# Second cross attention: the probability turn moved from TensorE to VectorE 32x32 transposes and SBUF-to-SBUF DMAs, attended values one context later

## The reference, cut to what matters

```
q, k, v = x @ Wq + bq,  ctx @ Wk + bk,  ctx @ Wv + bv      # 64 queries, 512 keys per context
score   = q k^T / sqrt(32) + mask * -1e9                    # per head: 64 x 512
attn    = softmax(score)                                    # over the 512 keys
x       = x + (attn v, heads side by side) @ Wo + bo
```

## Time and profile before

| what | value |
|---|---|
| median of three runs | 1252.92 us (1252.54 to 1254.14) |
| span of the profiled execution | 1248.6 us |
| TensorE busy | 1202.0 us (96%) |
| VectorE busy | 708.9 us (57%) |
| ScalarE busy | 520.2 us (42%) |
| GpSimd busy | 141.5 us (11%) |
| DMA traffic | 88.21 MB in 48485 packets, mean 71 GB/s |
| span of the 16 contexts, first score to last attended value | 399.7 to 881.8 us |

### The profile page before, as it was taken

How to read it: one execution, slowest core, us unless ns; L and a number is a source line. 1 busy time by engine, 2 the same in 40 slices (tenths; PEclk the granted TensorE clock), 3 DMA queues, 4 the chain that set the end, 5 groups by cost and what they waited for, 6 DMA issues and landing times.

```text
span 1248.6 us, 25643 instructions
## 1 busy us (share of the span) xinstructions
PE 1202.0 (96%) x10969; PEld 895.9 (72%) x10969; DVE 708.9 (57%) x1569; ACT 520.2 (42%) x1028; POOL 141.5 (11%) x164
## 2 busy tenths in 40 slices
PE   7999889999999999999999999999899999999997
PEld 5654478766466777777777777777787678888886
DVE  5456486767783555555555555555686755434432
ACT  3344447742132554545444444445453332222321
POOL 1300031166523000000000000000131100000000
PEclk9999999999999999999999999999999999999999
DMA  9669500201113110000010011110500201111210
GB/s 357 255 234 407 200 1 1 76 1 41 62 55 131 51 54 35 35 35 35 35 35 35 35 44 38 57 37 2 86 1 1 77 1 34 34 35 34 68 34 34
DMA packets 48485, 88.21 MB, mean 71 GB/s; under 512 B 19002, under 2 KB 20076, under 8 KB 44148
## 3 DMA queue, kind: packets, MB, share of 16 engines
q1 hardware_dynamic: 47024, 85.48, 19.4%
q10 hardware_dynamic: 1348, 1.09, 0.4%
HBM read 65.59 MB, written 20.97 MB: 69 GB/s over the span
## 4 chain that ended last, share of the span: by engine, by line
PE 88%; DVE 6%; ACT 3%; issue 1%; POOL 1%; DMA 1%; POOLq 0%; SPq 0%; DVEq 0%; ACTq 0%
PE bank L289 59%; PE bank L245 4%; PE bank L1790 3%; PE bank L1811 2%; PE bank L559 2%; PE bank L577 2%; PE bank L1138 2%; PE bank L1117 2%; PE bank L235 1%; DVE W L1380 1%; PE bank L495 1%; PE bank L2535 1%; PE bank L1086 1%; PE bank L1070 1%; PE bank L1094 1%
## 5 line engine op out<-in xcount | busy, mean ns | idle before, releaser
L2023 ACT ACTIVATE W<-W,low 128x512 f32<-128x512 f32 x128 | 90.9, 713 | 57.2 <-DVE low L1929 57.2
L2003 ACT ACTIVATE K<-bank,vecT 128x512 f32<-128x512 f32 x64 | 43.8, 689 | 167.0 <-PE bank L289 167.0
L225 POOL TENSOR_TENSOR rstd<-rstd,half_pow 128x1 f32<-128x1 f32 x48 | 30.9, 645 | 684.0 <-DVE rstd L221 684.0
L1902 DVE TENSOR_TENSOR W<-bank,vecT 128x256 f32<-128x256 f32 x16 | 6.8, 425 | 164.2 <-PE bank L1811 164.2
L1929 DVE CUSTOM_DVE_ANT_0 W<-bank,W 128x512 f32<-128x512 f32 x128 | 80.8, 687 | 30.6 <-PE bank L1790 30.6
L289 PE MATMUL bank<-xT,wT 128*128 128x512 f32 x384 | 92.8, 391 | 0.8 <-ACT W L2837 0.5
L289 PE MATMUL bank<-ctxT,Wkv 128*128 128x512 f32 x384 | 93.5, 396 | 0.0
L289 PE MATMUL bank<-Wq,Wkv 128*128 128x512 f32 x384 | 93.0, 394 | 0.0
L289 PE MATMUL bank<-Wkv,ctxT 128*128 128x512 f32 x384 | 92.9, 394 | 0.0
L289 PE MATMUL bank<-Wkv,Wq 128*128 128x512 f32 x384 | 92.1, 395 | 0.0
L289 PE MATMUL bank<-woT,hR 128*128 128x512 f32 x384 | 91.7, 394 | 0.1
(11 more groups left out here) (343 smaller groups left out, 2171.4 us busy)
## 6 DMA issues: line engine op xcount, KB each, us to landing
W<-ctx_turned SPq DMA_DIRECT2D x16, 1024.0 KB, 4.8
W<-in_ctx_dram SPq DMA_DIRECT2D x8, 1024.0 KB, 10.6
ctx_turned<-ctxT SPq DMA_DIRECT2D x8, 1024.0 KB, 7.6
ctx_turned<-W SPq DMA_DIRECT2D x8, 1024.0 KB, 6.6
XT<-in_ctx_dram SPq DMA_DIRECT2D x4, 1024.0 KB, 11.7
XT<-in_L_ffn_wi_dram SPq DMA_DIRECT2D x4, 1024.0 KB, 5.9
XT<-in_L_ffn_wo_dram SPq DMA_DIRECT2D x4, 1024.0 KB, 5.1
raw_own<-in_ctx_dram SPq DMA_DIRECT2D x3, 1024.0 KB, 10.7
```

The costliest lines, as they stand in the source:

```text
L225: pool.tensor_tensor(rstd[:, g:g + 1], rstd[:, g:g + 1], half_pow[:], ALU.pow).then_inc(rstd_ok.s, 1)
L2003: act.activation(K[:, m, :], bank[:, n % 4, :], ACT.Identity, bias=pcol("L1_xattn_bk", m)).then_inc(ring_a.s, 1)
L2023: act.activation(PR[:, j, :], PR[:, j, :], ACT.Exp, bias=low[:, j:j + 1], scale=-1.0, accum_out=total[:, j:j + 1]).then_inc(expd.s, 1)
```

## The change

1. TensorE no longer turns the probabilities: `probs_pe`, `turned_a` and their semaphores go. ScalarE's 8 copies per context go with them.
2. VectorE's 8 multiplications by the reciprocal per context go to GpSimd (`tensor_scalar`, 128x512). The 8 reciprocals of one column become 2 of four columns (`recips_v`).
3. VectorE turns each probability tile in place, in blocks of 32x32 (`dve.transpose`, 8 of 128x512 per context, in `probs_v`).
4. SP moves the blocks to their partitions: `move_probs(i, half)` issues 16 DMAs per half, 32 per context. Each takes 32 partitions and 16 runs of 32 elements (128 bytes) on each, from `PR` to `PT`: 512 runs and 64 KB per DMA, 2 MB per context. `scores_v(i + 1, 0)` and `(i + 1, 4)` on VectorE and `attend_pe(i)` on TensorE wait for them.
5. `attend_pe(i)` moves into the next pass, behind `scores_pe(i + 1, 1)`. Values get a second buffer (`slot(3)`). After the loop come rows, `key_weight_pe` and `attend_pe(15)`, which waits for the last 32 DMAs.
6. The order is adapted: the output stands behind the last values, `halves_a` and `halves_v` stand later in the pass, the bias additions on GpSimd stand behind the scaling of context 0, and `L1_attn_Wk` is loaded in the last context, into `V`. SP issues `load_context(i + 2)` ahead of `move_probs(i, ...)`, after it has waited for `context_v(i + 1, 3)`.

```diff
             USES = [("key", 0, m) for m in range(C)]
             for i in range(NI):
-                USES += [("value", i, k) for k in range(2)]
+                USES += [("value", i, 0)]
+                if i:
+                    USES += [("attended", i - 1, 0)]
+                USES += [("value", i, k) for k in range(1, KT)]
                 if i and i % 2 == 0:
                     USES += [("output", i // 2 - 1, 0)]
-                USES += [("value", i, k) for k in range(2, KT)]
                 if i < NI - 1:
                     USES += [("key", i + 1, m) for m in range(C)]
-                    USES += [("attended", i, 0)]
...
+            def move_probs(i, half):
+
+                sp.wait_ge(probs.s, probs(XPAIRS * i + 4 * half + 3))
+                if i:
+                    sp.wait_ge(ring.s, ring(use_of["attended", i - 1, 0]))
+                pairs = slice(4 * half, 4 * half + 4)
+                for q in range(4):
+                    rows, to = slice(32 * q, 32 * q + 32), slice(32 * q, 32 * q + 32)
+                    for r in range(4):
+                        strip = slice(32 * r, 32 * r + 32)
+                        sp.dma_start(PT[strip, pairs, :, to].rearrange("p t k n -> p (t k) n"),
+                                     PR[rows, pairs, :].rearrange("p t (k n) -> p (t k) n", n=P)[:, :, strip]
+                                     ).then_inc(pt_in[half].s, 16)
...
-                for i in range(1, NI - 1):
-                    sp.wait_ge(ctx_v.s, ctx_v(4 * i + 3))
-                    load_context(i + 1)
-                sp.wait_ge(ctx_v.s, ctx_v(4 * (NI - 1) + 3))
-                load_slot(4, "L1_attn_Wv")
-                sp.wait_ge(pt_pe.s, pt_pe(2 * NI - 1))
+                for i in range(NI):
+                    if i < NI - 1:
+                        sp.wait_ge(ctx_v.s, ctx_v(4 * (i + 1) + 3))
+                        if i < NI - 2:
+                            load_context(i + 2)
+                        else:
+                            load_slot(4, "L1_attn_Wv")
+                    else:
+                        sp.wait_ge(ring.s, ring(use_of["attended", i - 1, 0]))
+                        sp.dma_start(V[:], a["L1_attn_Wk"].rearrange("(c p) n -> p c n", p=P)).then_inc(slot_in[3].s, 16)
+                    for half in range(2):
+                        move_probs(i, half)
+                for half in range(2):
+                    probs_landed(sp, NI - 1, half)
                 load_slot(5, "L1_attn_Wq")
...
+                for i in range(NI):
+                    for t in range(XPAIRS):
+                        if t % 4 == 0:
+                            pool.wait_ge(recip.s, recip(2 * i + t // 4))
+                        pool.tensor_scalar(PR[:, t, :], PR[:, t, :], total[:, t:t + 1], None, ALU.mult).then_inc(scaled_p.s, 1)
...
                     scores_pe(i, 1)
+                    if i:
+                        attend_pe(i - 1)
                     values_pe(i, 1)
...
+                    if i and i % 2 == 0:
+                        output_pe(i // 2 - 1)
                     if more:
-                        keys_pe(i + 1, 0)
-                    probs_pe(i, 0)
...
+                        for m in range(C):
+                            keys_pe(i + 1, m)
+                pe.wait_ge(wt_v.s, wt_v(4))
+                for g in range(3):
+                    transpose_rows(xn5, 4, g, 5 + g)
+                key_weight_pe()
+                attend_pe(NI - 1)
...
             def scores_v(i, j):
                 dve.wait_ge(score.s, score(2 * i + j // 4))
-                if i:
-                    dve.wait_ge(pt_pe.s, pt_pe(2 * (i - 1) + j // 4))
+                if i and j % 4 == 0:
+                    probs_landed(dve, i - 1, j // 4)
...
+            def recips_v(i, half):
+                dve.wait_ge(expd.s, expd(XPAIRS * i + 4 * half + 3))
+                dve.reciprocal(total[:, 4 * half:4 * half + 4], total[:, 4 * half:4 * half + 4]).then_inc(recip.s, 1)
+
             def probs_v(i, j):
-                dve.wait_ge(expd.s, expd(XPAIRS * i + j))
-                dve.reciprocal(total[:, j:j + 1], total[:, j:j + 1]).then_inc(recip.s, 1)
-                dve.wait_ge(recip.s, recip(XPAIRS * i + j))
-                dve.tensor_scalar(PR[:, j, :], PR[:, j, :], total[:, j:j + 1], None, ALU.mult).then_inc(probs.s, 1)
+
+                dve.wait_ge(scaled_p.s, scaled_p(XPAIRS * i + j))
+                dve.transpose(PR[:, j, :], PR[:, j, :]).then_inc(probs.s, 1)
...
                     for t in range(4):
                         scores_v(i, t)
+                    for t in range(4, XPAIRS):
+                        scores_v(i, t)
+                    recips_v(i, 0)
+                    value_v(i, 0)
+                    if i:
+                        attended_v(i - 1)
+                    recips_v(i, 1)
+                    value_v(i, 1)
+                    for t in range(4):
+                        probs_v(i, t)
                     if j is not None:
                         halves_v(j)
...
                     for r in range(4):
                         if more:
                             context_v(i + 1, r)
                         else:
                             value_weight_v(r)
-                    for t in range(4):
+                    for t in range(4, XPAIRS):
                         probs_v(i, t)
+                    value_v(i, 2)
+                    value_v(i, 3)
...
-                    for n in range(4):
-                        turned_a(i, n)
...
-                    for n in range(4, 8):
-                        turned_a(i, n)
```

More of the change, by code:

```diff
@@ L1806, in attend_pe @@
                 taken_pe("value", i, KT - 1)
-                pe.wait_ge(pt_a.s, pt_a(XPAIRS * i + XPAIRS - 1))
+                for half in range(2):
+                    probs_landed(pe, i, half)
                 for c in range(C):
@@ L1888, in value_v @@
                 dve.wait_ge(ring.s, ring(n))
-                dve.tensor_copy(V[:, k, :], bank[:, n % 4, :]).then_inc(ring_v.s, 1)
+                dve.tensor_copy(values[i % 2][:, k, :], bank[:, n % 4, :]).then_inc(ring_v.s, 1)
             def attended_v(i):
@@ L1959, in vector @@
                         scores_v(i, t)
+                    for t in range(4, XPAIRS):
[8 more added lines that the diff above has]
+                        probs_v(i, t)
                     if j is not None:
                         halves_v(j)
-                    for t in range(4, XPAIRS):
-                        scores_v(i, t)
-                    value_v(i, 0)
-                    value_v(i, 1)
-                    if j is not None:
-                        output_v(j)
                     for r in range(4):
@@ L1993, in vector @@
                         split_v(wo[:, 1, :, :], W[:, 3, :, :], wo[:, 0, :, :]).then_inc(wt_v.s, 1)
+                for r in range(4):
+                    key_weight_v(r)
+                attended_v(NI - 1)
             def context_a(i, c):
@@ L2053, in scalar @@
                             value_weight_a(r)
-                    if more:
-                        key_a(i + 1, 0)
-                    for n in range(4):
-                        turned_a(i, n)
-                    if more:
-                        key_a(i + 1, 1)
-                        key_a(i + 1, 2)
-                    for n in range(4, 8):
-                        turned_a(i, n)
-                    if more:
-                        key_a(i + 1, 3)
-                    else:
-                        for r in range(4):
-                            key_weight_a(r)
+                    if i and i % 2 == 0:
+                        halves_a(i // 2 - 1)
                     if i == 0:
@@ L2071, in scalar @@
                         act.copy(wo[:, 0, :, :], W[:, 3, :, :]).then_inc(wt_a.s, 1)
+                    if more:
+                        for m in range(C):
+                            key_a(i + 1, m)
+                    else:
+                        for r in range(4):
+                            key_weight_a(r)
             sync()
```

77 lines of the change are left out of this document (19 added, 58 removed).

## The result

The changed kernel takes 1395.47 us in the median (1390.64 to 1397.67), the kernel before 1252.73: a ratio of 1.112, 95% interval 1.109 to 1.115. Forecast was 1237, in a range of 1222 to 1310. The profiled execution took 1397.67 us for a span of 1396.4, so the launch around the span adds 1.3 us, not the 4.3 that I had put down to it.

A forecast was written before the change was run, and what follows sets the result against it. TensorE was taken as the bound, with SP's moves near it: mean context 29.0 us, 24 less over 15, 1 less in context 0, 6.5 more at the end, -18.5; with waits and launch 1237, range 1222 to 1310.

The forecast's parts named there:

- What bounds the kernel: TensorE holds 88% of the chain; without the turns, 2.22 us less per context, mean 28.3 us instead of 30.55.
- The path: VectorE's fifth score through SP's moves to the next context's: 15.2 + 31x us in even contexts, about 14.5 + 31x in odd.
- x: SP's time to issue one of the 32 new DMAs: 0.45 us, bounds 0.30 and 0.75; even with today near 0.49.
- The engines' pace: DMA engines' cost of 512 short runs, read from the lora_B loads: 0.30 us, or 0.43 over the whole stream.
- GpSimd's scaling: Multiplying a 128x512 probability tile by its reciprocals on GpSimd: 0.95 us, bounds 0.49 and 1.25.
- rival 2: GpSimd and VectorE hold each other up, SP's start slips some 3 us per context: +23.5 us, 1276; chance 0.08.
- Transposes: VectorE's transpose of one probability tile: 0.61 us, bounds 0.40 and 1.3; first four done at about 7.8 us.
- Nothing late at 28.3 us: With the turns gone, no other engine makes TensorE wait at a mean context of 28.3 us: 33 us less over 15.
- rival 3: DMAs hidden, x at 0.38 or less, TensorE stays the bound everywhere: -31 us, 1222; chance 0.12.
- The end: Last context, `attend_pe(15)` waits uncovered for the last DMAs: 32 us from 25.6, 6.5 more than now.
- Rival 1: Moves become the bound at `scores_v` and `attend_pe`, x 0.50 or more: 1283 at 0.55, near 1380 at 0.75; chance 0.35.
- The two estimates drawn from DMA: Bandwidth & Descriptors of the Trainium skill: Moves per context: 69 us for 32 DMAs if not overlapped; some 6 us of DMA engines for 2 MB at 78%.

The follow-up runs named there:

- the better pair: Two contexts of the changed kernel with VectorE's order changed and ScalarE issuing 6 of each 16 DMAs (8 in the last context), SP 10: 1234.9 us, ratio 0.982.
- the wide run: Changed kernel with 8 DMAs of 128 partitions per context in place of 32 of 32 partitions, same bytes: 1263.5 us, ratio 1.006.
- two queues: Changed kernel with half of each 16 DMAs issued by ScalarE's queue instead of SP's: 1263.9 us, ratio 1.006.
- with `context_v` first: Changed kernel with half of the DMAs issued by ScalarE and `context_v` ahead of the first four transposes on VectorE: 1259.3 us, ratio 1.003.
- 24 issues on SP: Changed kernel with ScalarE issuing 8 of 32 DMAs, `context_v` and half split before the first transposes, values 2 and 3 before the last four: 1268.1 us, ratio 1.009.

## Why the prediction was wrong, point by point

- **What bounds the kernel**: right. Where the moves are hidden and the order is mended, the missing turns bring what they were said to bring: the better pair takes 56.3 us, 1.0 of it a wait, against the predicted 29.4 + 27.3 = 56.7, and the mean over 15 contexts is 28.5 us against 28.3.
- **The path** (SP's start + load + 31x + landing): right in form. Its terms in context 8 were 13.1, 0.4, 23.9 and 1.6; forecast were 12.3, 0.4, 14.4 (32 at 0.45) and 2.0 (2.5 less one issue). Each way of shortening it brought time back: SP's start earlier, half of the issues gone, 8 in place of 32. That 13.1 lies so near 12.3 is luck: the first four transposes were through 9.6 us after the fifth score, not 7.8, because the slow `attend_pe` (3.38 us) makes value 1 late, and the five splits took 3.5 us, not 4.5.
- **x, the step that failed.** I set 0.45 because a weight load, the conv_w load and a stream of row loads cost 0.43 to 0.47, and because I set the eight stores to `x_rows` at 0.75 aside for their split partitions. It measured 0.67 in a steady stream, 0.75 with the backlog behind the 1 MB load. The argument by shape was wrong: neither strides nor partitions move it much. And two of the three prices (weight load, conv_w load) were of a first issue, not of a stream. The rows to go by stood in the trace: the stores to `x_rows` are a stream out of SBUF, and even the 1 MB load behind them took 0.77 us, the maximum in the earlier trace rows. The first lora_B load took 0.66, too, but I read it as a queue that was already full. With x at 0.746 the forecast's own formula gives 15.2 + 23.1 = 38.3 us where 38.9 was measured; its row for 0.75 said 1380. The stores' issues (ns, min/median/max):

```profile
L1726 SPq DMA_DIRECT2D x_rows<-X x8: 576/606/877, 369.0 to 374.2; - x8
```

- **The engines' pace**: about right. 0.30 to 0.43 us per 512 runs were the two lora_B readings; the wide run shows 0.29 where the engines are full, and 13.35 / 32 = 0.42 with the load in the stretch.
- **GpSimd's scaling** was mis-sized: 1.57 us a tile in the median and 1.67 in the mean, outside my bounds of 0.49 to 1.25. It did not matter in the changed kernel, where scaling on VectorE was slower; once the DMAs were hidden it was worth 0.6 us in an odd context.
- **GpSimd and VectorE holding each other up** (rival 2): there, but smaller. Four `context_v` took 2.90 us with GpSimd at work and 2.50 without, 0.1 each, not 0.35. GpSimd lost more: the scaling that starts at 727.8, beside these four, took 2.36 us. Rival 2 had a chance of 0.08 for a mechanism that is worth under 1 us per context.
- **Transposes**: 0.61 us taken; right. Four take 2.67 us with a short wait for GpSimd, and one alone 0.69.
- **Nothing late at 28.3 us**: wrong, and hidden by the greater error. I gave "the copies of values 2 and 3" as the cover to watch and then set it to nothing. With the DMAs hidden by two queues or eight wide DMAs, TensorE waited 2.4 us for `context_v` in odd contexts and 1.0 to 1.2 for value 2 in even ones, and the time was 1.006 of the kernel before. So even with x at 0.38, my rival 3 with its 1222, the change as written would by these runs have brought nothing; no run has that x itself.
- **The end** was mis-sized: +25.0 us where I had +6.5. The last 32 issues start 23.5 us after the context's first score, not 13.6 (+9.9), because attended values 14 now wait 7.0 us for `PT` too, which I had left out, and `attend_pe` and the products behind it run slower. Issues and landing take 23.5 us instead of 16.5 (+7.0), which is x again. The last `attend_pe` takes 3.64 instead of 2.0 (+1.6). The output product behind it is slower as well (4.53 against 3.02).
- **Rival 1** was the case that came, with its mechanism, its place (`scores_v` and `attend_pe` waiting for `PT`) and nearly its price. My 0.35 for it was too low and my range ended at 1310, though its own upper bound gave 1380.
- The two estimates drawn from DMA: Bandwidth & Descriptors of the Trainium skill were both off. 32 DMAs did not cost 69 us, they overlapped; a small one lands 2.1 us after its issue, so the trace agrees with the Trainium skill's 2.0 us for one transfer (a fit to DMAs that GpSimd issues), and not with a sum of them. And by the engines' pace above, 2 MB in 128-byte runs took them some 9 to 13 us (32 times 0.29 to 0.42, an estimate), not 6; the Trainium skill's 78% is given for a 1 MB remote DMA, which this is not. Its rule that many small transfers should be coalesced agrees: eight in place of 32 took 132 us off.

## What to carry to other kernels

Count the DMAs, not only their bytes: here one queue issues a small one every 0.63 to 0.67 us, in every shape tried, so 32 in a 28 us period are a bound before the engines are. When the cost of an issue decides the sign, the dearest row of a small DMA in the trace belongs in the range, unless an experiment excludes it; and take the price of a stream from a stream, not from an issue that stands alone. And when work leaves the bounding engine, walk the order of every other engine at the new, shorter period: each instruction that waits holds up what stands behind it, and here three such orders hid one behind the other.

## What the runs showed of the hardware that I had not expected

- A GpSimd `tensor_scalar` of 128x512 with one scalar per partition takes 1.57 us in the median, 1.67 in the mean (13.31 for eight, held up by VectorE); its two-input `tensor_tensor` takes 1.04 to 1.25, and VectorE does the former in 0.49. One input instead of two did not make it cheaper.
- These small DMAs cost SP 0.59 to 0.63 us each to issue in a stream, from SBUF or from DRAM, over 32 or 128 partitions, in runs of 128 bytes or 2 KB. The 1 MB load from the same queue costs 0.33 behind a wait and 0.62 directly behind 16 small ones. Two queues at once need 0.68 and 0.70 us per issue (10.85 us for 16 on SP and 11.23 on ScalarE, with `context_v` first, context of 661.55), and 0.82 to 0.85 where the 1 MB load directly precedes them (13.06 and 13.57 us for 16).
- TensorE ran slowly after the long waits. The windows hold the wait for `PT` and the `attend_pe` behind it; after the five engines' busy times stand the granted clock, the DMA share and GB/s:

```profile
749.30:756.20 6.90, 0.00 (x1) 0.00 (x0) 0.00 (x0) 0.00 (x0) 0.00 (x0) 0.63 0.56 95
756.30:759.90 3.60, 3.60 (x129) 3.43 (x129) 3.19 (x10) 2.88 (x9) 0.89 (x1) 0.50 0.02 7
```

After 7 us without a matmul the granted clock is 0.50 (1.2 GHz), and `attend_pe` takes 3.6 us where it took 1.99 at 2.4 GHz. In the changed kernel this is about 1.5 us per context on top of the wait; over the next 4.1 us (759.9 to 764.0) the granted clock is 0.83. Shorter waits did not always do it: with 24 issues on SP, `attend_pe` took 1.99 us behind a wait of 2.73 us and 3.59 behind one of 2.79.
